# Cross-attention and expert layers on one core: attention inputs prepared a slot ahead, K and Q stacks by 6 writes and 4 reads, the gate with tokens as weights

## Chip, cores and metric

One core of one Trainium2 chip. The metric is device time in microseconds; the time of a version is the median of its runs.

## What is computed

```python
# x, ctx: (8, 256, 512) f32
h = layernorm(x, axis=-1)
q, k, v = Wq @ h + bq, Wk @ ctx + bk, Wv @ ctx + bv      # 256 channels = 16 heads of 16, 512 columns
p = softmax(scale * q^T k) per head                      # 512 x 512
x = x + tanh(g_xattn) * (Wo @ (p v) + bo)
# then, per token (a row of 512), 12 experts of width 320, the best 2 of each token:
t = layernorm(x);  logits = t @ gate_w.T;  cw = softmax weights of the top 2, renormalised
x = x + tanh(g_ffn) * sum_e cw[e] * (silu(t @ w1[e].T) * (t @ w3[e].T)) @ w2[e].T
```

## The kernel before

One program on one core. Its first part is attention, batch by batch, its second (routing, 43 tiles of 128 tokens by expert, an indirect scatter-add) works on all tokens.

**Slots.** Attention is a pipeline over 10 slots written out by `slots` (L343): in slot t (stage a) batch t is projected, (b_) batch t-1 has its scores, exponentials and products with V, (c) batch t-2 has its output projection, second normalisation and gate. Slots 2 to 7 are a loop of two. Slot 0 has only a, slot 1 a and b_, slot 8 b_ and c, slot 9 c. Each slot has 16 steps v (4 head groups by 4 blocks of 128 columns). In a step TensorE (`slot`, L1258) makes the two score groups of step v+1 (`scores`, two tiles S of 128x1024, each after the exponential that frees it), then the extra product that the table EXTRA (L322) puts there, then the products with V of step v (`values`, after the second exponential of step v). ScalarE makes two exponentials of 128x1024 in a step. The extra products are k0, k1, q0, q1 (a half of K or Q, 6 matmuls of 512 columns), v0, v1 (two blocks of V each), o0, o1 (output), t0, t1 (transposes of the normalised tokens), lg (gate logits as 12 x 256) and lt (their transposes through lgT).

**Products.** A projection uses weights and inputs split into a high and a low f16 part: three passes of two matmuls. VectorE makes the high part by a cast, GpSimd the low part by a subtraction (`lo_part`, L552, 2.1 us), and VectorE moves the results out of PSUM. All projections of a go through one PSUM tile MA, those of c through MC; each is used again only after VectorE has emptied it.

**K and Q.** Score matmuls contract over 49 rows: three blocks of 16 rows (K hi, hi, lo against Q hi, lo, hi) and a shift row. The stacks are built through DRAM: SP writes both parts of K (L469) and of Q (L471) with one DMA of 512 KB each, waits for both, and reads 12 blocks of 16 partitions x 8 KB in 1 KB runs (L480).

**Order on SP in a slot** (L425): load context and x of batch t; for c, row sums out of osum (L448), 4 of 8 moves of the sums of products, the inverse sums to DRAM (L453), the other 4, 8 broadcast reads of the inverse sums (L464); the writes and reads of K and Q; the stores of x and of the normalised tokens.

**Order on VectorE in a slot** (L812): bias into x (c); the quarter due at step 0; wait for the row sums, checks and reciprocal (L841, L843); cast of the context (L859), statistics of x (L861); then the steps: normalising x at step 2 (L886), the quotient at step 6 (L898), the evacuations, the token's second normalisation at step 11, osum after every fourth step (L965), and last the quarter due in this step.

**Quarters of expert weights.** Each of 12 experts has its weights split into f16 parts in four quarters (48 in all) beside attention: `split_quarter` (L791) on VectorE (L796, L798), and on ScalarE `store_quarter` (L665), which waits for the split, stores it and then issues the load of the quarter that uses the same buffer two quarters later (there are two buffers, c % 2). The store of a quarter split at step v stands behind the second exponential of step min(v + 2, 15):

```python
for v, e, c in splits:
    if u == 2 * min(v + 2, VS - 1) + 1:
        store_quarter(e, c)
```

A steady slot splits four, at steps 0, 5, 9 and 12; slot 0 four, slots 1 and 8 eight, slot 9 two, and the last two are split in the first expert tiles.

Of the kernel before, what the change touches and what calls it, by code (L numbers as in the profile page):

```python
# [14 lines left out]
P = 128  # L15
# [34 lines left out]
class Signals:  # L50


    def __init__(self, sem):
        self.xc = sem("xc")
# [38 lines left out]
def flamingo_kernel(nc, x, ctx_in, g_xattn, g_ffn, WqT, bq, WkT, bk, WvT, bv, WoT, bo, gateT, wall, out):  # L93
# [35 lines left out]
    q_dram = nc.dram_tensor("q_parts", [2, C, T], F16).ap()  # L129
    k_dram = nc.dram_tensor("k_parts", [2, C, T], F16).ap()  # L130
# [10 lines left out]
    with top:  # L141
# [13 lines left out]
        lgT = sb("lgT", [NE, C])  # L155
# [136 lines left out]
        s_rows = [sem(f"s_rows{i}") for i in range(2)]  # L292
        s_done = sem("s_done")

        def both_runs(eng, attention):
# [7 lines left out]
        NCONST2 = 3 + 3 + 1  # L303
# [14 lines left out]
        A_USES = {n: k for k, n in enumerate(("k0", "k1", "q0", "q1", "v0", "v1"))}  # L318
        C_USES = {n: k for k, n in enumerate(("o0", "o1", "t0", "t1", "lg", "lt"))}
# [6 lines left out]
        VS = GROUPS * TT  # L326

        def quarters(t):

            if t.i is None and t.add == 0:  # L330
                steps, experts = (4, 8, 11, 12), (0,)
            elif t.i is None and t.add == 1:
                steps, experts = (0, 2, 4, 6, 8, 10, 12, 14), (1, 2)
            elif t.i is None and t.add == B:
                steps, experts = (0, 2, 4, 6, 8, 10, 12, 13), (NE - 3, NE - 2)
            elif t.i is None and t.add == B + 1:
                steps, experts = (7, 7), (NE - 1,)
            else:
                steps, experts = (0, 5, 9, 12), (t.before(-1),)
            experts = [e if isinstance(e, At) else At(None, 0, e) for e in experts]  # L340
            return [(v, experts[n // 4], n % 4) for n, v in enumerate(steps)]

        def slots(eng, slot):  # L343

            slot(eng, At(None, 0, 0), 0, True, False, False)
            slot(eng, At(None, 0, 1), 1, True, True, False)
            with eng.Fori(0, (B - 2) // 2) as i:
                slot(eng, At(i, 2, 2), 0, True, True, True)
                slot(eng, At(i, 2, 3), 1, True, True, True)
            slot(eng, At(None, 0, B), 0, False, True, True)  # L350
            slot(eng, At(None, 0, B + 1), 1, False, False, True)
# [59 lines left out]
        def _(sp):  # L411
            sp.dma_start(w4[:, 0, :, :], WkT.rearrange("(k p) n -> p k n", p=P)).then_inc(s_const, 16)

            def attention(sp, g, guard):
# [4 lines left out]
                def load_batch(b, par):  # L419
                    sp.dma_start(ctx_sb[par][:, :, :],  # L420
                                 c_v[bass.ds(b.value(), 1)].rearrange("b p m t -> p (b m) t")).then_inc(g.xc, 16)
# [3 lines left out]
                def slot(sp, t, par, a, b_, c):  # L425
# [39 lines left out]
                    if a:  # L465

                        wait(sp, g.qk, t, 16 * 4 * PARTS, 0, s_bog)
                        wait(sp, g.kl, t, 1, 1)
                        sp.dma_start(k_dram.rearrange("h (m p) t -> p h m t", p=P), ks[:, :, :, :]).then_inc(g.qkst, 16)  # L469
                        wait(sp, g.ql, t, 1, 1)  # L470
# [34 lines left out]
            for n in range(2):  # L505
                sp.wait_ge(s_wst[n], 16 * 2 * (NE - 1))
            for e in range(EB // 2, NE):
# [7 lines left out]
                if e == NE - 1:  # L515
                    for n in range(2):
                        sp.wait_ge(s_wst[n], 16 * 2 * NE)
# [902 lines left out]
```

## Time and profile before

| | us |
|---|---|
| median of 3 runs | 808.91 (804.32 to 809.18) |
| the profiled execution | 802.83 |
| its span | 801.1 |

Times in rows are microseconds from the span's start, means of one instruction are ns. PE is TensorE's matmuls, PEld its weight loads, DVE VectorE, ACT ScalarE, POOL GpSimd, SP SyncE; a q behind the name (SPq, ACTq) is the engine's sequencer, which issues DMAs. "<-" behind a time in brackets names what ended the engine's idle time.

### The profile page before, as it was taken

The page shows a single profiled execution, that of the slowest core. Times are in us where ns is not written, and L with a number is a line of the kernel's source. Part 1 is how long each engine was busy: PE and PEld are TensorE (multiplying, and loading weights), DVE is VectorE, ACT ScalarE, POOL GpSimd, SP SyncE. Part 2 cuts the span into 40 slices and gives each one's busy share as a digit, 9 for nine tenths or more (in the row PEclk, how much of TensorE's full clock was granted, in tenths as well). Part 3 has the DMA queues.
Part 4 walks back from the last instruction along what each step waited for, and adds up shares of the span by engine and source line. Part 5 has one row for each costly group of instructions (what it writes and reads, how often), then busy time and mean ns, then how long its engine had stood idle before and what let it go on. Part 6 is the DMA issues. An engine that isn't in the chain of part 4 may idle for free.

```text
span 801.1 us, 14200 instructions
## 1 busy us (share of the span) xinstructions
PE 621.2 (78%) x4169; PEld 270.8 (34%) x4170; DVE 420.0 (52%) x769; ACT 332.0 (41%) x394; POOL 243.0 (30%) x186
## 2 busy tenths in 40 slices
PE   3418849889698897988976523179999999999993
PEld 1101202213122131322311101156666666666661
DVE  4787546667466574657646652944333333333330
ACT  5216637567565666665684200002222222222221
POOL 5203105133141332314202111324444333544322
PEclk9959969999999999999997755569999999999997
DMA  5686886967949688695894747527587776764533
GB/s 159 172 221 179 209 248 172 217 205 194 274 134 249 184 179 256 151 275 165 181 283 150 209 152 262 211 79 208 121 234 201 225 205 185 196 114 83 91 40 41
DMA packets 75374, 146.54 MB, mean 183 GB/s; under 512 B 10757, under 2 KB 36870, under 8 KB 73798
## 3 DMA queue, kind: packets, MB, share of 16 engines
q1 hardware_dynamic: 43664, 68.18, 31.4%
q10 hardware_dynamic: 22038, 55.35, 22.7%
q0 software_dynamic: 9632, 22.55, 14.9%
q8 instruction: 17, 0.28, 0.1%
q14 instruction: 23, 0.19, 0.1%
HBM read 87.85 MB, written 53.74 MB: 177 GB/s over the span
## 4 chain that ended last, share of the span: by engine, by line
PE 43%; DMA 19%; issue 16%; DVE 8%; POOL 5%; SPq 5%; ACT 1%; POOLq 0%; DVEq 0%; ACTq 0%
PE S L1334 15%; PE O L1355 9%; DMA K<-k_parts 8%; PE O L1198 5%; PE MA L1234 4%; DMA out<-yo,slot_out 4%; SPq L480 3%; PE S L1159 3%; DMA zl<-osum 2%; PE S L1321 2%; PE MC L1234 2%; DMA q_parts<-qs 2%; ACT prob L694 1%; PE S L1345 1%; POOL qs L552 1%
## 5 line engine op out<-in xcount | busy, mean ns | idle before, releaser
L694 ACT ACTIVATE prob<-S 128x1024 f32<-128x1024 f32 x256 | 245.8, 1024 | 179.8 <-PE S L1159 146.7
L1334 PE MATMUL S<-W,xT 128*128 x1032 | 149.4, 302 | 1.2 <-DVE xT L1107 1.2
L1198 PE MATMUL O<-prob,V 128*32 128x512 f32 x1024 | 148.1, 642 | 0.0
L1159 PE MATMUL S<-Q,K 49*128 49x512 f16 x512 | 91.4, 406 | 65.4 <-DMA K<-k_parts 42.2
L1334 PEld LDWEIGHTS S<-W,xT 128*128 128x128 f16 x1032 | 99.9, 99 | 38.7 <-issue 1.5
L620 POOL DMA_INDIRECT out<-yo,slot_out x43 | 68.5, 1593 | 116.9 <-DMA out<-yo,slot_out 60.0
L1355 PE MATMUL O<-W,hT 128*128 (+1 forms) x344 | 90.3, 381 | 0.9 <-DVE hT L1127 0.9
L1159 PEld LDWEIGHTS S<-Q,K 49*128 49x128 f16 x512 | 20.2, 94 | 193.6 <-ACT prob L694 135.4
L1115 DVE SCALAR_TENSOR_TENSOR hh<-S,act 128x320 f32<-128x320 f32 x43 | 21.1, 492 | 122.6 <-PE S L1334 122.6
L798 DVE SCALAR_TENSOR_TENSOR wp<-wf,wp 128x1024 f16<-128x1024 f32 x48 | 69.6, 1451 | 1.7
L552 POOL TENSOR_TENSOR cs<-ctx,cs 128x1024 f16<-128x1024 f32 x8 | 17.0, 2125 | 150.1 <-DVE cs L859 150.1
L596 POOL DMA_INDIRECT xg<-tokens_normed,slot_tok x43 | 42.6, 991 | 47.7 <-PE S L1321 35.3
L739 ACT ACTIVATE yo<-O,slot_w 128x512 f32<-128x512 f32 x43 | 29.6, 688 | 60.6 <-PE O L1355 60.6
L733 ACT ACTIVATE hs<-hh 128x320 f16<-128x320 f32 x43 | 20.2, 470 | 77.6 <-DVE hh L1115 77.6
L726 ACT ACTIVATE act<-S 128x320 f32<-128x320 f32 x43 | 18.8, 438 | 79.5 <-PE S L1334 79.5
L796 DVE TENSOR_SCALAR wp<-wf 128x1024 f16<-128x1024 f32 x48 | 41.2, 859 | 15.2 <-DMA wf<-wall 15.2
L1355 PEld LDWEIGHTS O<-W,hT 128*128 128x128 f16 (+1 forms) x344 | 31.6, 97 | 49.3 <-issue 29.0
L1234 PE MATMUL MA<-cs,w4s 128*128 128x512 f16 x96 | 28.3, 427 | 18.6 <-DVE kf L911 9.1
L1127 DVE COPY hT<-S 128x640 f16<-128x640 f16 x43 | 21.2, 492 | 41.0 <-PE S L1345 41.0
L552 POOL TENSOR_TENSOR os<-kf,os 128x1024 f16<-128x1024 f32 x8 | 17.8, 2229 | 77.1 <-DVE os L900 77.1
L1234 PE MATMUL MC<-os,w4s 128*128 128x512 f16 x96 | 27.6, 426 | 17.5 <-DVE os L900 13.7
L965 DVE COPY osum<-O 128x512 f32<-128x512 f32 x32 | 21.9, 685 | 30.0 <-PE O L1198 30.0
(153 smaller groups left out, 650.4 us busy)
## 6 DMA issues: line engine op xcount, KB each, us to landing
wf<-wall ACTq DMA_DIRECT2D x48, 512.0 KB, 7.1
weight_parts<-wp ACTq DMA_DIRECT2D x48, 512.0 KB, 4.7
W<-weight_parts SPq DMA_DIRECT2D x10, 2048.0 KB, 9.2
Q<-q_parts SPq DMA_DIRECT2D x48, 128.0 KB, 7.8
K<-k_parts SPq DMA_DIRECT2D x48, 128.0 KB, 8.2
ctx<-ctx_in SPq DMA_DIRECT2D x8, 512.0 KB, 12.5
residual<-x SPq DMA_DIRECT2D x8, 512.0 KB, 13.9
k_parts<-ks SPq DMA_DIRECT2D x8, 512.0 KB, 2.8
```

What stands on the lines that cost most here:

```text
L552: pool.tensor_tensor(parts[:, 1], f[:, :, :], parts[:, 0], ALU.subtract).then_inc(lo, 1)
L596: pool.indirect_dma_start(out=xg[j % TR][:, :], out_offset=None, in_=xn_dram[:, :], in_offset=bass.IndirectOffsetOnAxis(ap=slot_tok[:, j:j ...
L620: pool.indirect_dma_start(out=out[:, :], out_offset=bass.IndirectOffsetOnAxis(ap=slot_out[:, j:j + 1], axis=0), in_=yo[j % TR][:, :], in_o ...
L694: act.activation(prob[:, u % RING, :], S[u % 2][:, :], ACT.Exp, scale=SCALE).then_inc(g.exp, 1)
L739: act.activation(yo[n % TR][:, :], y_ps[:, :], ACT.Copy, scale=slot_w[:, bass.ds(j.value(), 1)])\
L796: dve.tensor_scalar(wp[c % 2][:, 0], wf[c % 2][:, :], WS, None, ALU.mult).then_inc(s_whi, 1)
L798: dve.scalar_tensor_tensor(out=wp[c % 2][:, 1], in0=wf[c % 2][:, :], scalar=WS, in1=wp[c % 2][:, 0], op0=ALU.mult, op1=ALU.subtract).then_ ...
L1159: last = pe.matmul(S[u % 2][:, s * T:(s + 1) * T], K[par][r0:r0 + PARTS * DK + 1, 2 * g4 + n, st * P:(st + 1) * P], Q[par][r0:r0 + PARTS * ...
L1198: last = pe.matmul(O[g4 % 2][2 * DK * j:2 * DK * (j + 1), :], V[par][:, st, GH * g4 + j, :], prob[:, u % RING, (j % 2) * T:(j % 2 + 1) * T ...
L1234: last = pe.matmul(bank[:, :], w4s[:, wp_, w, k, m * P:(m + 1) * P], src[:, xp, k, :], start=(n == 0 and k == 0), stop=(n == len(PASSES) - ...
L1334: last = pe.matmul(ps, xT[par][:, xp * TT + k, :], W[:, bass.ds(off + (w * WCOL + (2 * k + n) * F), F)], start=(k == 0 and (xp, w) == (0, 0)),
L1355: last = pe.matmul(y_ps[:, :], hT[par][0:rows_, block, :], W[0:rows_, bass.ds(off + (w * WCOL + W2 + k * T), T)], start=(n == 0), stop=(n ...
```

## The change

It does six things.

1. The pipeline gets a fourth stage p: in slot t the context and x of batch t+1 are loaded, x is normalised (statistics at step 6, values at step 8) and the context is cast (step 11). The loads have a semaphore each. Batch 0 is prepared before slot 0. The order on SP in a slot is now: loads of batch t+1, sums, K and Q, stores.
2. K, Q, V products move to steps 0 to 6 and 10, V in four pieces; the quotient goes to step 5, the second output product is cut in two halves (steps 8 and 9), the second normalisation goes to step 10. The extra product stands between the two score groups of a step. VectorE waits for the row sums at step 1 and takes the reciprocal before the range checks.
3. K and Q: 6 writes of 256 KB (one for each row block, each as soon as its part is there) and 4 reads of 48 partitions in 2 KB runs. The order of the heads changes with it (`head`), and Wo is loaded in 8 blocks. The shift row is used only in the second, guarded version of attention, so its 8 fills go from the main path.
4. The gate: tokens are the stationary operand, 8 products of 12 columns that give the logits directly; lt and lgT go.
5. Quarters: none in slots 0 and 9 and in the tiles, four in slot 1 (steps 4, 7, 11, 13), six in a steady slot (2, 4, 7, 11, 12, 13), eight in slot 8 as before.
6. At the start: context first, then Wk, then x; Wq and its biases ahead of Wv and Wo; the splits of Wk and Wq before slot 0; GpSimd's constants after the first low parts.

```diff
-        EXTRA = {3: "k0", 4: "k1", 5: "q0", 7: "q1", 8: "o0", 9: "v0", 10: "o1", 11: "v1", 12: "t0", 13: "t1",
-                 14: "lg", 15: "lt"}
-        ON_AT, XN2_AT, SPLIT_AT = 6, 11, 6
+        EXTRA = {0: "k0", 1: "k1", 2: "q0", 3: "q1", 4: "v0", 5: "v1", 6: "v2", 7: "o0", 8: "o1a", 9: "o1b",
+                 10: "v3", 12: "t0", 13: "t1", 14: "lg"}
+        ON_AT, LN_AT, XN_AT, XN2_AT, CS_AT, SPLIT_AT = 5, 6, 8, 10, 11, 3
...
         def quarters(t):
...
-                steps, experts = (0, 5, 9, 12), (t.before(-1),)
+                steps = (2, 4, 7, 11, 12, 13)
...
# SP, slot
-                    if a:
-
-                        wait(sp, g.xc, t, 32, 0, s_bog)
-                        wait(sp, g.a_free, t, NA, -NA)
-                        load_batch(t, par)
+                    if p:
+
+                        nxt = t.before(-1)
+                        wait(sp, g.cc, nxt, 16, 0, s_bog)
+                        wait(sp, g.xc, nxt, 16, 0, s_bog)
+                        wait(sp, g.cl, nxt, 1, -1)
+                        load_ctx(nxt, 1 - par)
+                        load_x(nxt)
...
+                        for stack, parts, dram, hi, lo, order in ((K, ks, k_dram, g.kh, g.kl, (0, 0, 1)),
+                                                                  (Q, qs, q_dram, g.qh, g.ql, (0, 1, 0))):
+                            wait(sp, hi, t, 1, 1)
+                            for r in sorted(range(PARTS), key=lambda r: order[r]):
+                                if order[r] == 1:
+                                    wait(sp, lo, t, 1, 1)
+                                sp.dma_start(dram[:, r], parts[:, order[r]].rearrange("p m t -> p (m t)"))\
+                                    .then_inc(g.qkst, 16)
...
+                        for stack, dram in ((K, k_dram), (Q, q_dram)):
+                            for s in range(2):
+                                sp.dma_start(stack[par][64 * s:64 * s + PARTS * DK, :, :]
+                                             .rearrange("p (g m) t -> p g (m t)", m=CT),
+                                             dram.rearrange("(g s) r c n -> s (r c) g n", s=2)[s]).then_inc(g.qk, 16)
...
# TensorE, slot
                     for v in range(VS):
                         if b_ and v + 1 < VS:
-                            scores(bb, 1 - par, v + 1)
-                        what = EXTRA.get(v)
+                            scores(bb, 1 - par, v + 1, (0,))
+                        what = EXTRA.get(v, "")
                         if a and what in A_USES:
                             project(t, par, what)
-                        if c and what in C_USES:
+                        if c and what[0:2] in C_USES:
                             output(bc, what)
+                        if b_ and v + 1 < VS:
+                            scores(bb, 1 - par, v + 1, (1,))
```

The DRAM tensors of K and Q parts are now `[8, 3, 16, 1024]` (heads in pairs of halves, row block, row, both halves of the columns' channels), so that `dram[:, r]` is 8 runs of 16 x 1024 values.

## Rows read from the trace of the kernel before

**Rows 1.** The page, part 4: shares of the chain that ended last, by engine.

```profile
PE 43%; DMA 19%; issue 16%; DVE 8%; POOL 5%; SPq 5%; ACT 1%; POOLq 0%; DVEq 0%; ACTq 0%
```

**Rows 2.** Busy time by stage: slots 0, 1, 4, 8, slot 0's end.

```profile
core 0: us, PE busy (x) PEld busy (x) DVE busy (x) ACT busy (x) POOL busy (x), PEclk, DMA share, GB/s
0.00:55.20 55.20, 16.68 (x52) 6.72 (x53) 36.29 (x43) 15.94 (x6) 15.24 (x24) 0.85 0.71 195
55.20:110.80 55.60, 37.72 (x232) 9.41 (x232) 32.21 (x38) 30.38 (x32) 10.18 (x6) 0.84 0.75 196
206.60:255.30 48.70, 40.19 (x270) 11.79 (x266) 30.67 (x50) 30.82 (x32) 14.61 (x10) 1.00 0.78 202
401.40:449.80 48.40, 36.51 (x220) 8.39 (x218) 29.68 (x39) 30.43 (x32) 6.88 (x4) 0.86 0.72 219
42.00:55.20 13.20, 0.00 (x0) 0.00 (x0) 10.63 (x5) 0.00 (x0) 0.00 (x0) 0.50 1.07 294
```

**Rows 3.** Timeline of slot 0: start, us, instruction, idle before it.

```profile
19.49 2.72 PE L1234 MATMUL MA<-xs,w4s 128*128 128x512 f16 x6 [0.89 <-issue]
...
20.75 3.02 DVE L798 SCALAR_TENSOR_TENSOR wp<-wf,wp 128x1024 f16<-128x1024 f32 x1
...
31.51 0.36 SPq L471 DMA_DIRECT2D q_parts<-qs  x1
...
34.29 0.33 SPq L480 DMA_DIRECT2D Q<-q_parts  x1
...
55.23 1.03 PE L1159 MATMUL S<-Q,K 49*128 49x512 f16 x4 [20.38 <-DMA K<-k_parts]
```

**Rows 4.** Timeline of a steady slot (slot 5), the same columns.

```profile
255.84 3.77 ACT L694 ACTIVATE prob<-S 128x1024 f32<-128x1024 f32 x4 [2.63 <-PE S L1159]
...
258.37 1.93 PE L1198 MATMUL O<-prob,V 128*32 128x512 f32 x8
...
265.35 2.13 POOL L552 TENSOR_TENSOR cs<-ctx,cs 128x1024 f16<-128x1024 f32 x1 [17.53 <-DVE cs L859]
...
268.76 3.59 SPq L464 DMA_DIRECT2D ocz<-inverse_sums  x8
...
273.33 0.61 PE L1159 MATMUL S<-Q,K 49*128 49x512 f16 x4
...
273.87 1.47 PE L1234 MATMUL MA<-xs,w4s 128*128 128x512 f16 x6
...
275.27 1.06 PE L1198 MATMUL O<-prob,V 128*32 128x512 f32 x8
...
276.78 1.94 ACT L694 ACTIVATE prob<-S 128x1024 f32<-128x1024 f32 x2 [0.99 <-PE S L1159]
...
279.64 1.94 ACT L694 ACTIVATE prob<-S 128x1024 f32<-128x1024 f32 x2 [0.92 <-PE S L1159]
...
304.34 0.73 PE L1159 MATMUL S<-Q,K 49*128 49x512 f16 x4 [1.92 <-DMA K<-k_parts]
```

**Rows 5.** DMA queues, 276:279 (first) and 255.3:304.2: packets, MB, share.

```profile
q1 hardware_dynamic: 528, 0.52, 49.3%
...
q10 hardware_dynamic: 1659, 4.18, 28.5%
```

**Rows 6.** Groups of the same slot, then the tile wf over the span.

```profile
L798 DVE SCALAR_TENSOR_TENSOR wp<-wf,wp 128x1024 f16<-128x1024 f32 x4 | 4.9, 1226 | 0.1
L796 DVE TENSOR_SCALAR wp<-wf 128x1024 f16<-128x1024 f32 x4 | 3.7, 932 | 0.0
...
DMA to landing us min/median/max: 4.1/7.1/13.8
```

**Rows 7.** Timeline of slot 9, then its chain in order of time.

```profile
470.78 1.03 PE L1234 MATMUL MC<-os,w4s 128*128 128x512 f16 x2 [0.63 <-POOL os L552]
...
473.58 0.74 DVE L935 SCALAR_TENSOR_TENSOR residual<-MC,cols,residual 128x512 f32<-128x512 f32 x1
...
484.41 8.10 DMA tokens_normed<-xs
```

More of the change, by code:

```diff
@@ L334, in quarters @@
             elif t.i is None and t.add == B:
-                steps, experts = (0, 2, 4, 6, 8, 10, 12, 13), (NE - 3, NE - 2)
-            elif t.i is None and t.add == B + 1:
-                steps, experts = (7, 7), (NE - 1,)
-            else:
-                steps, experts = (0, 5, 9, 12), (t.before(-1),)
-            experts = [e if isinstance(e, At) else At(None, 0, e) for e in experts]
-            return [(v, experts[n // 4], n % 4) for n, v in enumerate(steps)]
-        def slots(eng, slot):
[L345 to L351, printed above, removed]
+                steps = (0, 2, 4, 6, 8, 10, 12, 13)
@@ new lines, in quarters @@
+            return [(v, e, c) for v, (e, c) in zip(steps, parts)]
+        def slots(eng, slot):
+            slot(eng, At(None, 0, 0), 0, True, False, False, True)
+            slot(eng, At(None, 0, 1), 1, True, True, False, True)
+            with eng.Fori(0, (B - 4) // 2) as i:
+                slot(eng, At(i, 2, 2), 0, True, True, True, True)
+                slot(eng, At(i, 2, 3), 1, True, True, True, True)
+            slot(eng, At(None, 0, B - 2), 0, True, True, True, True)
+            slot(eng, At(None, 0, B - 1), 1, True, True, True, False)
+            slot(eng, At(None, 0, B), 0, False, True, True, False)
+            slot(eng, At(None, 0, B + 1), 1, False, False, True, False)
@@ L1147, in attention, with scores @@
             def attention(pe, g, guard):
-                def scores(b, par, v):
+                def scores(b, par, v, halves=(0, 1)):
                     g4, st = divmod(v, TT)
-                    if v == 0:
-                        wait(pe, g.qk, b, 16 * 4 * PARTS, 16 * 4 * PARTS)
-                    for n in range(2):
+                    if v == 0 and 0 in halves:
+                        wait(pe, g.qk, b, KQ_READS, KQ_READS)
+                    rows_ = PARTS * DK + (1 if guard else 0)
+                    for n in halves:
                         u = 2 * v + n
@@ L1230, in three @@
                             wait(pe, hi, b, 1, 1)
-                        if first and xp == 1:
+                        if first and xp == 1 and k == 0:
                             wait(pe, lo, b, 1, c)
-                        for k in range(CT):
-                            last = pe.matmul(bank[:, :], w4s[:, wp_, w, k, m * P:(m + 1) * P], src[:, xp, k, :],
-                                             start=(n == 0 and k == 0), stop=(n == len(PASSES) - 1 and k == CT - 1))
+                        last = pe.matmul(bank[:, :], w4s[:, wp_, w, k, m * P:(m + 1) * P], src[:, xp, k, :],
+                                         start=(n == 0), stop=(n == 3 * CT - 1))
                     return last
                 def output(b, what):
-                    wait(pe, g.c_free, b, NCU, C_USES[what] + 1, s_bias if what == "lt" else None)
-                    if what[0] == "o":
-                        m = int(what[1])
-                        last = three(MC, 3, m, os_, b, g.oh, g.ol, m == 0, 2)
-                    elif what[0] == "t":
-                        m = int(what[1])
+                    name, part = what[0:2], what[2:]
+                    n0, n1 = {"": (0, 3 * CT), "a": (0, 3), "b": (3, 3 * CT)}[part]
+                    if n0 == 0:
+                        wait(pe, g.c_free, b, NCU, C_USES[name] + 1)
+                    if name[0] == "o":
+                        m = int(name[1])
+                        last = three(MC, 3, m, os_, b, g.oh, g.ol, m == 0, 2, n0, n1)
+                    elif name[0] == "t":
+                        m = int(name[1])
                         wait(pe, g.xn2, b, CT, m + 1)
```

392 lines of the change are left out of this document (204 added, 188 removed).

## Prediction, made before the changed kernel was run

> **What bounds the kernel now.** I read the stages by windows first, then the chain, then a steady slot's timeline. The page's chain [rows 1] says that TensorE is on the path for 43% of the span and DMA for 19%. The windows [rows 2] give the stages: slot 0 takes 55.2 us with 16.68 us of TensorE work, slot 1 55.6 us, a steady slot 48.7 us (the one shown had the full clock and 40.19 us of TensorE work, 30.82 of exponentials, 30.67 of VectorE), slot 8 48.4 us. From 110.8 to 401.4 us six steady slots take 290.6 us, 48.4 us each. Routing, the expert tiles and the tail (from 491.5 us on) are not touched but for one expert's last two quarters.
>
> So no engine fills a steady slot. The timeline of one [rows 4] shows what does. VectorE waits for the row sums, casts the context only behind them, and GpSimd's low part of the context begins at 265.35 us, ten into the slot, after 17.53 us idle. K and Q are projected after that, written, read back, and the next slot's first scores at 304.34 us wait 1.92 us for K. A chain as long as the slot, not an engine, sets the period. In slots 0 and 1 the same chain is bare: the first scores come at 55.23 us after 20.38 us of waiting for K [rows 3].
>
> **Slot 0, -13 us.** The products for Q ended at 22.2 us (19.49 + 2.72), but VectorE was then in a 3.02 us split [rows 3]: no quarter is split in slot 0 now, which gives back 1.5 us; the context cast and the K weights no longer wait for x, about 1 us more. The last write of Q moves from 31.51 to some 29 us. The writes become six of 256 KB. A write of 512 KB in 1 KB packets took 49.3% of a 3 us stretch on 16 engines [rows 5], 1.5 us; K and Q together are 1.5 times as many bytes, but the last write is only half of the old one: 3 us to landing, as from 31.51 to 34.29 before, so the reads start at 32.3 us. Before, from the first read to the first scores it took 20.9 us (34.29 to 55.23) [rows 3], with a quarter's traffic and the next batch's loads beside it. Now these loads are done earlier, the packets are 2 KB and the DMAs four. Bounds: 20.9 us if none of that helps and, from below, 6 us, since 1.6 MB at the 294 GB/s of 42.0 to 55.2 us [rows 2] is 5.4 us. I take 9.7 us, nearer to the lower end because the loads beside it, 1 MB, and a quarter's 1 MB are more than the reads themselves: slot 0 ends at 42 us.
>
> The Trainium skill ("SBUF — State Buffer", the DMA port swizzle) says that the ports reached depend on the partitions of a transfer, eight partitions a port at 27.2 GB/s: 16 partitions reach 4 ports, 48 reach 8. By that the old reads need 14.5 us and the new ones 7.2, and slot 0 would end at 40 us. Against the change speaks "DMA: Bandwidth & Descriptors" (how many engines): the count divides the slowest dimension of both sides, which for the new writes is 8 on the DRAM side, so they would run on 8 engines, and the last write would take 0.7 us longer. No row here shows either.
>
> **Slot 1, -12.6 us.** Its K and Q products start at step 0 instead of step 3, since their inputs are ready; nothing waits for row sums. With q1 at step 3 the round trip fits in the remaining steps, so the wait for K at the end goes. What is late next is the pace. A step without a product is two exponentials (four in 3.77 us, so 1.88); one with a K, Q or output product is 0.54 + 1.40 + 1.00 = 2.94 us [rows 4]. Slot 1 has 4 of these (11.8), four V quarters at about 2.24 (9.0), eight bare steps (15.0): 35.8 us. A store and load issued on ScalarE stretches a bare step to 2.86 us (276.78 to 279.64) [rows 4]: 3.3 us for three bare steps and one with V. The clock is at its lower level after the idle stretch; a step there costs 1.03 (scores at 55.23) + 2.72 + 1.9 = 5.6 us [rows 3, 4] instead of 2.94, and part of the next: 3.9. Sum 43.0 against 55.6.
>
> **Slots 2 to 7, +1.6 us each.** TensorE's work is 40.2 us [rows 2]; the gate with tokens as weights replaces 4 products of 256 columns and two transposes by 8 products of 12 columns. Bounds 1 us either way; I take -0.7 (the turn through the narrow tile goes): 39.5. Extra products between the two score groups let ScalarE have its next input 1.4 us sooner, which keeps TensorE busy but doesn't shorten its work. Splits go from 4 to 6 quarters in a slot: each is 0.93 + 1.23 us on VectorE [rows 6] and one store and load on ScalarE. Their stores fall in steps 4, 6, 9, 13, 14, 15, none of which has a 1.40 us product: 3 x 0.6 (V and half-output steps) + 0.7 + 0.1 + 1.0 = 3.6 us. VectorE then has 34.5 us of work and holds up two things: V's third quarter behind the product of sums (1 us) and the second transpose behind two splits in steps 11 and 12 (1.7 us). Subtotal 45.8, rounded to 45.9.
>
> Then the term that speaks against the change. The sixth split is at step 13, and its buffer is the one of step 11: its load is issued by ScalarE only with the store of step 13. It lands 7.1 us later in the median, 4.1 to 13.8 [rows 6]; I take 6.5, since the reads are over. The split ends at 6.5 + 1.9 = 8.4 us after the issue. ScalarE's store of step 15 waits for it and stands in front of the next slot's exponentials. ScalarE gets there after four exponentials (4.1), another issue (1.0) and some 0.6 us of waiting: 5.7. So it stalls 2.7 us per slot, TensorE behind it idles, and its clock may drop for the next 6 us as at 258.37 us, where values took 1.93 instead of 1.06 us [rows 4]: 2.7 us if it does, 0 if it doesn't (it didn't in the slot at 206.6, whose clock was 1.00 [rows 2]); I take half. 45.9 + 2.7 + 1.4 = 50.0 us, against 48.4: +9.6 us for six. The row sums' wait hides inside this stall. DMA: the ACT queue's four quarters took 28.5% of a 48.9 us slot [rows 5], so six take 20.9 us of 50, seven more on a slot that had a DMA share of 0.78 [rows 2]: 0.9, close to full.
>
> **Slot 8, -2 us:** the same eight splits; the sums' round trip (output products had to wait for it) now runs without the tail of the reads; bounds -5 to +2 (the output product is a step earlier, so it can wait longer). **Slot 9, -4 us:** no split stands before the residual (it began at 473.58, its product was done at 471.81) and the two weight loads no longer start beside the last token store, which took 8.10 us [rows 7]; bounds -6 to -1. **Tiles:** the two quarters that go were hidden by TensorE's tiles: 0.
>
> **Sum.** 801.1 - 13.2 - 12.6 + 9.6 - 2 - 4 = 778.9 us of span; the profiled execution was 802.83 us, 1.7 above its span, so 780.6; the median of the runs is 808.91, 1.0076 times it: **787 us**.
>
> **Rivals.** (A) The forecast, 787; with the clock and load terms at their ends (48 to 53 us a slot) 774 to 805. (B) The late load costs nothing, because ScalarE and VectorE are themselves late when it lands: 45.9 us a slot, 3 x 6 = 15 less instead of 9.6 more: 762. For it: a load at the fast end, 4.1 us, would end the wait 2.4 us earlier, nearly all of the stall, and then no clock is lost. Against: the median is 7.1 us. (C) Slower: the queues are over-full at the slot's end. Context, x, the token store and a quarter's store are all in flight at step 13, and the load lands as the slow ones, 11.2 to 13.8 us [rows 6], 4.7 to 7.3 later than I took; at 55.5 us a slot the six cost 42.6 and all the gains (31.8) are eaten: 820. It decides from 53.7 us a slot, a landing of 10.2 us. For it: 0.9 of DMA share. Against: the reads of K and Q are over by step 12, so fewer transfers are beside this load than beside those issued late in a slot before. (D) The early preparation doesn't take the round trip off the slot's end, because the writes of K stand in SP's queue behind 17 transfers of sums (the last at 268.76 + 3.6, 15 us into the slot [rows 4]): slots as before, 48.4, and only the ends gain: 777. Against: 30 us remain for a round trip of 20.
>
> **How the numbers follow.** Chances: A 0.50, B 0.25, C 0.12, D 0.06, something else 0.07. Range for 8 in 10: from 757, a little below B, to 812, between A's end and C. A measurement tells about 1% from no change, so faster means under 800.8: nine tenths of A, all of B and D: 0.77. Within 1%: 0.13. Slower: C less its lower part: 0.10.
>
> **What would show it.** First exponential at about 42 us and the second batch's at 85; no wait for K at slot ends; a wait of scores' exponentials on a store issue at each slot's end, 2 to 3 us, with VectorE idle for the load before the last split; six slots of about 50 us. Wrong would be: reads of K and Q over 14 us, slots of 46 us or less (B), or loads landing over 10 us at step 13 (C).

## The result, and the profile after

The changed kernel took 819.4 us in the median of 4 runs (814.3 to 822.0); the kernel before, beside it on the same chip, 809.0. The ratio is 1.014, 95% interval 1.008 to 1.020: slower, where 787 us and faster were forecast. The profiled execution has a span of 812.5 us, 11.4 more than before; it was the fastest of the four runs. In a_spread three of the four runs and in x_dmaspr four of the eight, each time with the profiled one among them, took over 1.5% longer than the kernel's fastest run, so the slot figures of these two are the least sure.

I cut both spans at VectorE's last copy of row sums in each slot (osum), the same mark for all kernels below. "Rest" is slot 9, the routing, the tiles and the tail; slot 0 goes to the first exponential, slot 1 from there to its last copy.

| kernel | slot 0 | slot 1 | slots 2 to 7 | slot 8 | rest | span |
|---|---|---|---|---|---|---|
| before | 55.9 | 58.6 | 289.1 | 48.3 | 349.2 | 801.1 |
| after | 46.6 | 45.6 | 324.2 | 57.2 | 338.9 | 812.5 |

The ends gave what was hoped for, 9.3 + 13.0 + 10.3 us; the six steady slots took back 35.1 and slot 8 took 8.9. The six of both kernels, by windows (columns: engine busy time and instructions, granted TensorE clock, DMA share, GB/s). Before:

```profile
114.50:403.60 289.10, 249.81 (x1620) 72.14 (x1618) 184.22 (x302) 184.89 (x193) 87.71 (x60) 0.97 0.78 203
```

After:

```profile
92.20:416.40 324.20, 273.28 (x1656) 88.07 (x1654) 215.37 (x312) 188.67 (x191) 86.65 (x56) 0.89 0.79 227
```

Read TensorE first. Its work at full clock is the same: 249.81 x 0.97 = 242 and 273.28 x 0.89 = 243. Its idle time grew by 11.6 us (39.3 to 50.9); the other 23.5 of the 35.1 us are the same products at a lower granted clock, between the levels of 1.2 and 2.4 GHz. This is a division of time, not a price of the clock. The same stretch of two kernels below, a_oldq (the quarters of before) and x_both (hardly any split work and traffic), has slow products too, at 0.94 and 0.91, and these filled time in which TensorE had stood idle before:

```profile
110.10:400.00 289.90, 261.95 (x1657) 83.61 (x1656) 192.00 (x288) 190.94 (x194) 95.08 (x56) 0.94 0.76 214
90.50:374.40 283.90, 267.73 (x1656) 87.19 (x1656) 162.44 (x312) 189.62 (x193) 84.42 (x56) 0.91 0.58 137
```

With 12 and 18 us more of busy time than the kernel before, their six slots took 0.8 us more and 5.2 us less than its 289.1.

Where the stalls are, in the slot that answers to [rows 4] (255.3 to 310.4; the timeline of VectorE, GpSimd and ScalarE, start and duration first, in brackets the idle time before):

```profile
289.63 0.69 DVE L956 CAST xs<-xn 128x1024 f16<-128x1024 f32 x1
290.25 0.69 DVE L832 CAST cs<-ctx 128x1024 f16<-128x1024 f32 x1
290.85 0.68 DVE L964 COPY osum<-O 128x512 f32<-128x512 f32 x1
291.45 2.03 DVE L812 TENSOR_SCALAR wp<-wf 128x1024 f16<-128x1024 f32 x1
293.51 3.02 DVE L814 SCALAR_TENSOR_TENSOR wp<-wf,wp 128x1024 f16<-128x1024 f32 x1
...
306.82 0.69 DVE L812 TENSOR_SCALAR wp<-wf 128x1024 f16<-128x1024 f32 x1 [7.23 <-DMA wf<-wall]
...
290.41 2.52 POOL L596 TENSOR_TENSOR xs<-xn,xs 128x1024 f16<-128x1024 f32 x1 [1.85 <-DVE xs L956]
292.89 2.57 POOL L575 TENSOR_TENSOR cs<-ctx,cs 128x1024 f16<-128x1024 f32 x1
...
296.75 0.56 ACTq L697 DMA_DIRECT2D weight_parts<-wp  x1
297.47 0.53 ACTq L691 DMA_DIRECT2D wf<-wall  x1
298.18 1.94 ACT L716 ACTIVATE prob<-S 128x1024 f32<-128x1024 f32 x2 [5.12 <-issue]
...
309.00 0.56 ACTq L697 DMA_DIRECT2D weight_parts<-wp  x1
310.45 1.94 ACT L716 ACTIVATE prob<-S 128x1024 f32<-128x1024 f32 x2 [4.00 <-PE O L1229]
```

Two stalls stand there. **At step 11** VectorE casts two tiles, GpSimd subtracts twice behind the casts (290.41 to 295.46), and VectorE's split of a quarter lies across both: its two instructions take 2.03 and 3.02 us instead of 0.69 and 1.23. ScalarE's store (296.75) waits for that split in front of the exponentials: 5.12 us. **At step 13** the load issued at 297.47 lands some 9 us later, VectorE stands idle for 7.23 us, the split ends at 308.8, the store goes out at 309.00 and only then the next slot's exponentials run. The second is the late load of the forecast, with a slower landing; of the first the forecast had only 1.7 us for the transposes. Both splits are slow because of GpSimd: free ones take 0.69 and 1.23 us, and these two ended 0.55 and 1.07 us behind GpSimd's instructions, so they did most of their work only when those were over. Over the page (busy, mean ns, idle before; the last row the median landing):

```profile
L812 DVE TENSOR_SCALAR wp<-wf 128x1024 f16<-128x1024 f32 x48 | 48.6, 1012 | 48.9 <-DMA wf<-wall 48.9
L814 DVE SCALAR_TENSOR_TENSOR wp<-wf,wp 128x1024 f16<-128x1024 f32 x48 | 71.4, 1488 | 1.7
...
wf<-wall ACTq DMA_DIRECT2D x48, 512.0 KB, 7.1
```

VectorE's waits for loads rose from 15.2 us to 48.9. TensorE's and ScalarE's side of the same, the waits of slots 2 to 7 (total, times, longest), TensorE's for the transposes' copy before and after, ScalarE's after:

```profile
PE MC L1254 <- DVE xT L938: 7.0, 6, 1.2
...
PE MC L1280 <- DVE xT L933: 22.5, 6, 4.4
...
ACT prob L716 <- issue: 42.4, 12, 5.3
```

At the start, against [rows 3]: the last write of Q goes out at about 28.7, the reads at 33.25 and 34.12, and the first scores run at 45.92.

```profile
33.25 0.83 SPq L498 DMA_DIRECT2D K<-k_parts  x2
34.12 0.93 SPq L498 DMA_DIRECT2D Q<-q_parts  x2
...
35.17 0.40 SPq L432 DMA_DIRECT2D ctx<-ctx_in  x1
35.61 0.47 SPq L436 DMA_DIRECT2D residual<-x  x1
...
45.92 1.03 PE L1190 MATMUL S<-Q,K 48*128 48x512 f16 x4 [8.96 <-DMA Q<-q_parts]
```

### The profile page after: what moved, and what is told of

It is laid out like the page before. It is cut to its first block, busy times and chain, and to the rows that moved or that the text cites. A ratio compares the mean times of both kernels' runs of the same rounds, so it can differ in the third digit from the quotient of the medians.

```text
span 812.5 us, 13989 instructions
## 1 busy us (share of the span) xinstructions
PE 652.7 (80%) x4217; PEld 292.9 (36%) x4218; DVE 418.1 (51%) x757; ACT 324.0 (40%) x391; POOL 244.2 (30%) x186
## 3 DMA queue, kind: packets, MB, share of 16 engines
q10 hardware_dynamic: 22150, 55.35, 20.2%
## 4 chain that ended last, share of the span: by engine, by line
PE 48%; DMA 15%; DVE 15%; issue 11%; POOL 4%; SPq 3%; ACTq 1%; ACT 1%; DVEq 0%; POOLq 0%
PE S L1367 15%; PE O L1388 9%; PE O L1229 7%; DMA wf<-wall 5%; PE MA L1264 5%; PE S L1190 4%; DMA out<-yo,slot_out 3%; DVE wp L812 3%; DMA zl<-osum 2%; DVE wp L814 2%; PE S L1354 2%; PE MC L1284 2%; DMA ocz<-inverse_sums 1%; DMA Q<-q_parts 1%; PE MA L1246 1%
## 5 line engine op out<-in xcount | busy, mean ns | idle before, releaser
L716 ACT ACTIVATE prob<-S 128x1024 f32<-128x1024 f32 x256 | 252.1, 1025 | 207.9 <-PE S L1190 129.7
L1229 PE MATMUL O<-prob,V 128*32 128x512 f32 x1024 | 155.0, 682 | 0.0
L1190 PE MATMUL S<-Q,K 48*128 48x512 f16 x512 | 107.3, 425 | 43.7 <-ACT prob L716 33.0
L1190 PEld LDWEIGHTS S<-Q,K 48*128 48x128 f16 x512 | 24.3, 94 | 205.4 <-ACT prob L716 133.2
L812 DVE TENSOR_SCALAR wp<-wf 128x1024 f16<-128x1024 f32 x48 | 48.6, 1012 | 48.9 <-DMA wf<-wall 48.9
L814 DVE SCALAR_TENSOR_TENSOR wp<-wf,wp 128x1024 f16<-128x1024 f32 x48 | 71.4, 1488 | 1.7
L575 POOL TENSOR_TENSOR ks<-kf,ks 128x1024 f16<-128x1024 f32 x8 | 17.1, 2131 | 143.6 <-DVE ks L908 143.6
L761 ACT ACTIVATE yo<-O,slot_w 128x512 f32<-128x512 f32 x43 | 29.6, 688 | 60.6 <-PE O L1388 57.9
L1246 PE MATMUL MA<-w4s,cs 128*128 128x256 f16 x192 | 29.0, 291 | 16.1 <-DVE V L913 11.7
L1264 PE MATMUL MC<-os,w4s 128*128 128x512 f16 x96 | 28.9, 428 | 12.7 <-DVE os L890 11.0
L1280 PE MATMUL MC<-ident,xn 128*128 128x128 f32 x64 | 14.1, 360 | 27.3 <-DVE xT L933 23.3
```

The source lines that it names most:

```text
L575: pool.tensor_tensor(parts[:, 1], f[:, :, :], parts[:, 0], ALU.subtract).then_inc(lo, 1)
L716: act.activation(prob[:, u % RING, :], S[u % 2][:, :], ACT.Exp, scale=SCALE).then_inc(g.exp, 1)
L812: dve.tensor_scalar(wp[c % 2][:, 0], wf[c % 2][:, :], WS, None, ALU.mult).then_inc(s_whi, 1)
L814: dve.scalar_tensor_tensor(out=wp[c % 2][:, 1], in0=wf[c % 2][:, :], scalar=WS, in1=wp[c % 2][:, 0], op0=ALU.mult, op1=ALU.subtract).then_ ...
L1190: last = pe.matmul(S[u % 2][:, s * T:(s + 1) * T], K[par][r0:r0 + rows_, 2 * g4 + n, st * P:(st + 1) * P], Q[par][r0:r0 + rows_, 2 * g4 + ...
L1229: last = pe.matmul(O[g4 % 2][2 * DK * j:2 * DK * (j + 1), :], V[par][:, st, head(g4, j), :], prob[:, u % RING, (j % 2) * T:(j % 2 + 1) * T ...
```

## The experiments

The question was why a steady slot takes 54.0 us (324.2 / 6) where 48.2 were needed before. The slot figures below are all of this kind, from each kernel's one profile; the medians are of all its runs. Runs of one kernel differ by some 8 us, so a difference of 1 us in a slot (6 us over six) tells nothing.

**a_spread, a_noint, a_oldq, b_late: the place, the order or the number of the quarters.** The edits:

```
a_spread:  -steps = (2, 4, 7, 11, 12, 13)   +steps = (0, 3, 5, 8, 10, 13)
a_noint:   -scores(bb, 1 - par, v + 1, (0,)) ... scores(bb, 1 - par, v + 1, (1,))
           +scores(bb, 1 - par, v + 1)      (the product behind both groups)
a_oldq:    the quarters of before: slot 0 (4, 8, 11, 12), slot 1 eight, slots 2 to 7 (0, 5, 9, 12),
           slot 8 eight, slot 9 (5, 6, 7, 8)
b_late:    kernel before:  -steps = (0, 5, 9, 12)   +steps = (0, 11, 12, 13)
```

> The changed kernel with the same six quarters in a steady slot, split at steps 0, 3, 5, 8, 10, 13 instead of 2, 4, 7, 11, 12, 13, so that each load has two steps or more between its issue and its split. Theory T (the place of the quarters: the load for the split at step 13 is issued at step 13, and a second pile-up on VectorE at step 11): a slot goes from 54.4 to 49 to 51 us, the whole from 819 to 788 to 798, and ScalarE no longer waits for the store at a slot's end. Rival N (six quarters are too many for the engines and the DMA, wherever they stand): a slot stays at 53.5 us or more and the whole at 814 or more. Rival G (products between the score groups, the gate's new form, or the new writes and reads of K and Q are what lengthens the slot): as rival N, within 3 us of 819.

> The changed kernel with the extra product of a step again behind both score groups of the next step, nothing else. Theory T: the slot's length is set by the waits at steps 11 and 13, so the order of products inside a step does little: 816 to 822. Rival G in the form that the products between the groups cost (exponentials now come singly): a slot loses 1.5 us or more of its 54.4, the whole is under 811. If the order gains what its place suggests (ScalarE has its next input 1.4 us sooner), taking it away costs 3 to 10 us: 822 to 829.

> The changed kernel with the quarters laid out as before the change: 4 in slot 0 (steps 4, 8, 11, 12), 8 in slot 1, 4 in each of slots 2 to 7 at steps 0, 5, 9, 12, 8 in slot 8 and 4 in slot 9 (steps 5 to 8). Everything else of the change stays. Theory T and rival N both: a steady slot falls from 54.4 to 47 us or less, the six by 44 us or more, slots 0, 1 and 9 give back some 15: 785 to 795. Rival G: a slot stays at 51 us or more and, with slots 0, 1 and 9 longer, the whole is 812 or more.

> The kernel before with its four quarters of a steady slot split at steps 0, 11, 12, 13 instead of 0, 5, 9, 12, nothing else: the same number of quarters, but the load for the last one is issued at step 13, as in the changed kernel. Theory T: a slot gets 3 to 6 us longer than its 48.35, the whole goes from 809 to 827 to 845, with the wait for a store at the slot's end. Rival N: the number is the same, so the time is: within 4 us of 809.

a_spread: 819.7 us (806.7 to 822.7), 55.6 us a slot. Even its fastest run lies above the 798 that theory T allowed: T as I had put it fell. a_noint: 822.5 us, ratio 1.023 (1.016 to 1.031), 55.9 a slot: the products between the score groups cost nothing; if anything they gain some 3 us, which the intervals do not separate. a_oldq: 805.1 us, ratio 1.000 (0.997 to 1.004), 48.3 a slot, with slot 0 at 55.7 and slot 1 at 54.4. Everything else of the change (early preparation, writes and reads, gate) is in it, so rival G fell for the steady slots: the 5.7 us came with the two extra quarters and their new steps. But those parts gained nothing there either, 289.9 us for the six against 289.1, and the whole lies between what T and N said (785 to 795) and what G said (812). Of a_oldq's 12 quarters in slots 0 and 1, eight more than in the changed kernel, the cost is (55.7 + 54.4) - (46.6 + 45.6) = 17.9 us, 2.2 each. b_late: 844.0 us, ratio 1.046 (1.039 to 1.054), 55.4 a slot with only four quarters. So three late steps are worth 7.2 us a slot, where I expected 3 to 6. They hold two things, a late load and three splits in a row; TensorE's waits in the six slots (112.8 to 444.9) have both, 34.9 us for the copy behind the split that waits for its load and 20.2 us for the transposes' copy (7.0 before):

```profile
PE MC L1250 <- DVE lgT L940: 34.9, 6, 6.7
PE MC L1247 <- DVE xT L938: 20.2, 6, 3.4
```

Its VectorE rows, with split times as before the change and a wait for the load:

```profile
319.39 1.23 DVE L798 SCALAR_TENSOR_TENSOR wp<-wf,wp 128x1024 f16<-128x1024 f32 x1
329.38 0.69 DVE L796 TENSOR_SCALAR wp<-wf 128x1024 f16<-128x1024 f32 x1 [8.17 <-DMA wf<-wall]
```

So by these profiles six quarters at well-spaced steps cost as much as six at bad ones, and four at bad steps as much as both. What they share had to be found.

**x_dve, x_dma, x_store, x_pool: one resource taken away at a time.**

```
x_dve:    both instructions of a split on [0:64] of 1024 columns
x_dma:    loads wf[:, 0:64] (not the first two), stores of 64 columns (not expert 0's); experts read expert 0's parts
x_store:  only the stores cut, as in x_dma
x_pool:   GpSimd's subtractions on [..., 0:32] of 512 columns
(x_dve and x_pool fill the rest of the parts with zeros once at the start)
```

> The changed kernel with the two VectorE instructions of a split cut from 1024 to 64 columns (the experts' weights are then mostly not split; all loads, stores, their order and their waits stay). Two theories of why a steady slot takes 54 us with six quarters and 48 with four. Theory V (VectorE is late: splits of 1.9 us, stretched to 3.7 where GpSimd subtracts beside them, stand in front of what the products and ScalarE's stores wait for): the slots fall to 45 to 48 us, 36 us or more for the six. Theory D (DMA: the traffic of 1 MB a quarter and the landing of the loads): the slots stay above 52 us.

> The changed kernel with the loads and stores of quarters cut to 64 of 1024 columns, except the first two loads and the stores of expert 0 (the experts then all read the first one's parts; the same issues on ScalarE, the same work on VectorE). Theory D: the slots fall to 46 to 48 us. Theory V: the loads are never late any more, which takes off the 2 to 3 us of the wait for the last load, but VectorE's stretched splits stay: 50 to 52 us a slot.

> The changed kernel with only the stores of quarters cut to 64 columns (except those of expert 0; all experts read its parts). Half of the added traffic goes. Theory D in the form of bandwidth: a slot falls by 3 us or more, the median landing of the loads from 7.1 to under 5.5 us. Theory V: under 2 us a slot.

> The changed kernel with GpSimd's subtractions of the low parts cut from 512 to 32 columns each (the low parts are then mostly zero; six memsets of GpSimd are added at the start). Theory V with the lock between GpSimd and VectorE as its main part: no split instruction takes over 1.3 us, VectorE's busy time falls by 9 us or more a slot and a slot to 49 to 51 us. If the lock is a side matter: a slot stays above 52.5 us. Theory D: above 53.

x_dve: 813.7 us, ratio 1.007 (1.003 to 1.012), 55.6 a slot: against theory V as far as it is the splits' own work, for the hold-up by GpSimd stays (below). x_dma: 784.7 us, ratio 0.972 (0.966 to 0.979), 50.9 a slot: against D, inside what V said. x_store: 797.0 us, 52.9 a slot, median landing 6.5, so not D in the form of bandwidth (3 us or more and under 5.5). x_pool: 810.3 us, ratio 1.005 (1.001 to 1.009), 55.1 a slot, above the 52.5 that I had set for "a side matter", though its split instructions are all free of GpSimd:

```profile
L818 DVE SCALAR_TENSOR_TENSOR wp<-wf,wp 128x1024 f16<-128x1024 f32 x48 | 58.8, 1225 | 1.7
L816 DVE TENSOR_SCALAR wp<-wf 128x1024 f16<-128x1024 f32 x48 | 32.9, 686 | 63.4 <-DMA wf<-wall 63.1
```

The waits in the last row tell where the gain went: the time won on VectorE was waited for the loads, 63.1 us in place of 48.9 (in x_dve 70.6). The loads also landed later, 8.2 us in the median and in x_dve 8.9, for 7.1; why was not tried. x_dve also shows that the stretch has nothing to do with the size of the split: at step 11 even 64 columns took 1.53 and 2.08 us, 1.35 and 1.85 more than free ones (0.18 and 0.23), where 1024 columns took 1.34 and 1.79 more. They end right behind GpSimd's instructions (295.57 + 2.52 = 298.09, 298.06 + 2.11 = 300.17).

```profile
296.61 1.53 DVE L814 TENSOR_SCALAR wp<-wf 128x64 f16<-128x64 f32 x1
298.18 2.08 DVE L816 SCALAR_TENSOR_TENSOR wp<-wf,wp 128x64 f16<-128x64 f32 x1
```

```profile
295.57 2.52 POOL L596 TENSOR_TENSOR xs<-xn,xs 128x1024 f16<-128x1024 f32 x1 [1.85 <-DVE xs L958]
298.06 2.11 POOL L575 TENSOR_TENSOR cs<-ctx,cs 128x1024 f16<-128x1024 f32 x1
```

The Trainium skill states this in "SBUF — State Buffer" (SBUF: two separate sides): VectorE, in an instruction of a two-port mode or with two inputs from SBUF, and GpSimd share a pair of ports by an exclusive lock, and whichever starts second is blocked until the first is through. The trace agrees: a 0.18 us instruction took 1.53.

**a_lfirst, a_lfspr, c_mix, b_lfirst: the load ahead of its store.** ScalarE issued a quarter's store and then the next load into the same queue.

```
a_lfirst, b_lfirst:   -act.dma_start(w_dram[...], wp[...])   load_quarter(e, c + 2)
                      +load_quarter(e, c + 2)   act.dma_start(w_dram[...], wp[...])
a_lfspr:              the same, steps (0, 3, 5, 8, 10, 13)
c_mix:                the same; slot 0 none, slot 1 eight, slots 2 to 5 (0, 5, 9, 12), slots 6 and 7 (0, 2, 5, 7, 9, 12),
                      slot 8 eight, one quarter in slot 9 at step 7, three behind the first three tiles
```

> The changed kernel with the two DMAs that ScalarE issues for a quarter in the other order: the next load first, the store behind it (both in one queue, 512 KB each). Theory D in the form of landing (a load lands late because it stands behind its own store in the queue): the median landing falls from 7.1 to 5.5 us or less, the stalls of the step-13 load shrink by 1.5 us or more a slot, and the whole goes from 819 to 810 or less. Theory D in the form of bandwidth (16 DMA engines share out what is in flight): the landing stays within 0.7 us and the time within 4 us of 819.

> The changed kernel with both: loads issued before stores, and the six splits at steps 0, 3, 5, 8, 10, 13. With loads of 5.5 us or less each one is there when its split's turn comes (two or three steps of 3 us), so the landing form of theory D says 50 us or less a slot and 795 or less in all. The bandwidth form: as a_spread, 815 to 822.

> A version made to beat both: the changed kernel, loads before stores, four quarters at steps 0, 5, 9, 12 in slots 2 to 5, six in slots 6 and 7 (0, 2, 5, 7, 9, 12), eight in slots 1 and 8, none in slot 0, and of the last expert one quarter in slot 9 and three behind the first three tiles, where VectorE, ScalarE and the DMAs have room. By the stages measured so far: slot 0 47, slot 1 54, slots 2 to 5 48 each, 6 and 7 53 each, slot 8 54, the rest 341 to 344: 794 to 798 of span, 798 as the median; if the order of load and store also tells, 790.

> The kernel before with only the order of load and store turned round. Four quarters in a slot at steps 0, 5, 9, 12 leave their loads at least 7 us, so both forms of theory D say little: landing form 802 to 807 against 809, bandwidth form the same as before within 3 us.

a_lfirst: 814.1 us, ratio 1.009 (1.005 to 1.013), median landing 5.7 for 7.1: the loads did stand behind their stores, but little over half of the expected 9 us came, and in its profile the steady slots took 54.0 us as before. VectorE's waits before a split were now for an earlier store to leave its buffer, 45.5 us where it had waited 48.9 for loads. b_lfirst: 802.6 us, ratio 0.995 (0.992 to 0.999), landing 5.5: a swap of two lines that makes the kernel before a little faster. a_lfspr: 812.1 us, 54.5 a slot: with loads in time, the spread layout was still no good. c_mix: 809.4 us, far above the 798 expected: slots 6 and 7 took 54.9 each, and slot 9 with the routing was 75.5 us long with its one quarter, against 70.2 in c_t4 below without it, while three quarters behind the tiles cost 1.5 us (261.9 to 260.4).

**x_both, x_dmaspr, c_t4, c_t11: both at once, and the tiles.**

```
x_both:    x_dve and x_dma together
x_dmaspr:  x_dma with steps (0, 3, 5, 8, 10, 13)
c_t4:      as c_mix, nothing in slot 9, the last expert's four quarters behind tiles 0 to 3
c_t11:     the last eleven quarters behind tiles 0 to 10; slot 1 (2, 5, 8, 11, 14), slots 2 to 7 (0, 5, 9, 12), slot 8 eight
```

> The changed kernel with both cuts together: the two split instructions on 64 of 1024 columns, and loads and stores of quarters of 64 columns (except the first two loads and the stores of expert 0). With VectorE's part alone cut a steady slot stayed at 55.6 us, with the DMAs' part alone at 50.9. Theory S (a slot's end is late by the later of two things, VectorE behind its splits and the loads' landing, so only both cuts together free it): 45 to 47 us a slot, 276 or less for the six. Theory D (only the DMAs count): 50 to 51 us, as with the DMAs' cut alone.

> The changed kernel with small loads and stores as before and the six splits at steps 0, 3, 5, 8, 10, 13; VectorE's work is whole. Theory S: without traffic the place of the splits counts, since nothing is then late but VectorE at steps 11 to 13: 47 to 49 us a slot against 50.9 with the change's steps, and with full traffic (54.5 to 55.6 in this place) the rest is the DMAs' share: 6 us a slot for six quarters, 1 us each. If VectorE's total work (six splits of 2.5 us) is what binds: 50.5 or more.

> Loads before stores, four quarters in slots 2 to 5, six in 6 and 7, eight in 1 and 8, none in 0 and 9, and the last expert's four quarters behind the first four tiles. The earlier version with one quarter in slot 9 and three in the tiles took 809.4 us; its slot 9 and routing were 9.5 us longer than with no quarter there, its tiles 1 us. Both theories: that goes, 798 to 802. If a quarter costs its 3 us in the tiles too: 807 or more.

> The same with the last eleven quarters behind the first eleven tiles, so that five are in slot 1, four in each of slots 2 to 7 and eight in slot 8. By stages: slot 0 46, slot 1 46, the six 290, slot 8 52, slot 9 and routing 66, tiles and tail 275: 775 us of span, 777 as the median, if a quarter is free in the tiles (six steps of 1 us each there). If it costs 3 us there: 800. For this routing the experts come late enough; a routing that needs the last two experts in the first tiles would have to wait for them, so this run shows what the place is worth.

x_both: 762.0 us, 47.3 a slot. Alone the cuts moved a slot by +1.6 and -3.1 us, together by -6.7: theory S, one stall hides the other. What x_both takes away on VectorE is the splits' own work; in slots 2 to 7, 17 of its 72 split instructions still lose 22.5 us beside GpSimd's. x_dmaspr: 809.8 us (797.8 to 816.0), ratio 0.998 (0.994 to 1.003), 55.0 a slot, where S said 47 to 49. With hardly any traffic the spread layout was 4 us a slot worse than the change's own, and even its fastest run is 13 us above x_dma's 784.7, so its limit is not the traffic. Its timeline has what I take for the reason, four times in a slot; here step 10:

```profile
298.01 0.69 DVE L957 CAST xs<-xn 128x1024 f16<-128x1024 f32 x1
298.62 0.69 DVE L813 TENSOR_SCALAR wp<-wf 128x1024 f16<-128x1024 f32 x1
299.34 3.03 DVE L815 SCALAR_TENSOR_TENSOR wp<-wf,wp 128x1024 f16<-128x1024 f32 x1
```

```profile
298.78 2.51 POOL L596 TENSOR_TENSOR xs<-xn,xs 128x1024 f16<-128x1024 f32 x1 [1.85 <-DVE xs L957]
```

VectorE's cast releases GpSimd's subtraction, and a split in the same step stands right behind the cast: it is held up nearly every time. Between 85 and 480 us, 25 split instructions were stretched in a_spread, by 43.7 us in all; some 20 and 27 us in the changed kernel, some 10 and 11 before, none in x_pool. My spread steps 3, 5, 8 and 10 were the very steps with a cast. But a stretch costs only where something waits for it: in slots 2 to 7, a_oldq has 22.5 us of it and c_t11 22.6, as much as the changed kernel (23.7), and their slots took 48.3 and 47.7 us. In a_oldq TensorE waited only 3.9 us in all for the transposes' copy.

c_t4: 802.4 us, ratio 0.995 (0.991 to 0.999). c_t11: 785.6 us, ratio 0.976 (0.971 to 0.981): 47.7 a slot, and the tiles 270.8 us for 260.4, so eleven quarters cost 10.4 us there, 0.9 each, against 2 to 3 in the slots. This layout relies on a routing in which the last experts come late.

**a_clear and c_clear4: steps without a cast.**

```
a_clear:   a_lfirst with steps (0, 2, 4, 7, 9, 13)
c_clear4:  a_clear; slot 1 (4, 7, 10, 13), slot 8 (0, 4, 9, 13), the last expert's four quarters behind tiles 0 to 3
```

> The changed kernel with loads before stores and the six splits at steps 0, 2, 4, 7, 9, 13: at none of these does VectorE cast something in the same step (K at 1, Q at 3, the attention output at 5, x at 8, the second x at 10, the context at 11), so GpSimd's subtraction of 2.1 to 2.6 us is over before the split begins, and each load has two steps or more. Theory L (the splits stand right behind a cast, whose subtraction on GpSimd locks them out; late loads are the other half): no split instruction over 1.3 us for most, VectorE's busy time 6 us less a slot than in a_lfspr, and a slot falls from 54.5 to 48 to 50 us, the whole from 812 to 780 to 790. Theory S alone (VectorE's total or the traffic of six quarters binds, wherever they stand): 53 us or more a slot, 808 or more in all.

> The version before with slot 8 relieved: loads before stores, six splits in each of slots 2 to 7 at steps 0, 2, 4, 7, 9, 13, four in slot 1 (4, 7, 10, 13), four in slot 8 (0, 4, 9, 13), and the last expert's four quarters behind the first four tiles. Against 795.3 us: slot 8 gets 6 to 10 us shorter (four quarters less), slot 9 and the tiles 4 us longer together, as in c_t4 (3.7 and 0.8): 789 to 793. If VectorE's order and the loads are what counts, slots 2 to 7 stay at 51 to 52 us. If the gain of the version before was chance, they go back to 54 and the whole to 805.

a_clear: 795.3 us, ratio 0.989 (0.984 to 0.994), 51.6 a slot: the first layout of six quarters that beats the kernel before; against the changed kernel only the place of the splits and the order of two DMAs are new. It stopped 1.6 us a slot above what theory L said (48 to 50), and 795.3 is above its 780 to 790. Against a_lfspr, with the same order of DMAs, VectorE was busy for 29.6 us less in the six slots (230.8 to 201.2) and the slots were 17.5 us shorter. That it is the hold-up by GpSimd and not other work of VectorE at the same steps was not tried apart: no run took GpSimd's subtractions from the spread layout. The rows of its page and its waits in slots 2 to 7:

```profile
L814 DVE SCALAR_TENSOR_TENSOR wp<-wf,wp 128x1024 f16<-128x1024 f32 x48 | 62.4, 1300 | 1.7
L812 DVE TENSOR_SCALAR wp<-wf 128x1024 f16<-128x1024 f32 x48 | 42.5, 885 | 13.6 <-DMA weight_parts<-wp 13.2
```

```profile
ACT prob L716 <- issue: 9.1, 4, 4.0
```

ScalarE's waits in front of a store fell from 42.4 us to 9.1, and VectorE's before a split from 48.9 to 13.6, nearly all for a store to free its buffer. What is late next stands in TensorE's waits of the same stretch:

```profile
PE MA L1246 <- DVE V L913: 19.9, 6, 4.6
...
PE MA L1264 <- DVE kf L901: 8.2, 5, 4.1
```

The copies of V come late behind the split of step 4, which stands in front of them in VectorE's order, and those of K behind the wait for the row sums. c_clear4: 787.8 us, ratio 0.978 (0.972 to 0.984), 51.7 a slot, slot 8 40.6 us, slot 9 and routing 68.1. It holds for any routing: a token goes to two different experts, so at least half of all pairs, hence over four tiles, come before the last expert's. It and c_t11 are the best versions found, equal within the intervals.

## Why the prediction was wrong

**The direction came from the steady slots.** The sum said 45.9 + 2.7 + 1.4 = 50.0 us; 54.0 were measured, which over six slots is 24 of the 34 us that separate the forecast span (778.9) from the real one.

- *The stall by the late load, 2.7 us* (landing 6.5): the mechanism was right, the size was not. In the slot shown the load took 9.3 us, VectorE stood for 7.23, ScalarE for 4.00; over the six slots the load of step 13 took 6.8 to 11.6 us. b_late, with its three splits in a row, was 7.2 us a slot longer. Rival C named this at 0.12, with its point at 10.2 us of landing; one of the six loads reached that. That the time it gave, 820, came true is luck, because the next term failed too. Nor were the queues over-full: the DMA share of the six slots was 0.79, not 0.9.
- *VectorE's hold-ups, 1 + 1.7 us, and splits at 0.93 + 1.23 each*: this is the step that failed. The 0.93 of [rows 6] already mixed free instructions (0.69 us) with one that stood beside GpSimd's; the 1.23 was that of free ones. I carried both over to a layout that puts a split right behind the context cast moved to step 11. There the pair took 5.05 us, and TensorE waited 3.8 us a slot for the transposes' copy, ScalarE 5.12 us for the store, a wait that the sum put at nothing. No rival named it. How the missing 4.0 us divide between this term and the load's is open, because they hide each other: x_pool, with no split held up, got nothing back. That both together are the cause is what x_both (47.3) and, with whole work and traffic, a_clear (51.6) show.
- *The clock, 1.4 us*: the granted clock of the six went from 0.97 to 0.89, 23.5 us of slow products or 3.9 a slot. What of it lengthened the slots is not shown: x_both had 0.91 and slots of 47.3 us.
- *Rival B* (the load is hidden behind others' lateness, 762) was half right and in the wrong sense: the two do hide each other (x_dve, x_pool), but as two full stalls, not as none. That x_both took 762.0, B's own number, is luck: it also leaves out 53 us of VectorE's work in the six slots.

**Slot 0, -13 us**: -9.3. The writes landed at 33.2 instead of 32.3; the reads took 12.7 us (33.25 to 45.92), not 9.7. From 35 us on the DMAs were busy for over 0.9 of the time, and from 36 to 45 us they moved 135 to 182 GB/s, where my lower bound had 294. The Trainium skill's rule ("SBUF — State Buffer", the DMA port swizzle) gives an estimate of 7.2 us for the reads, further off than my 9.7; 1 MB of other loads was queued behind them. **Slot 1, -12.6**: right, -11.4 by first exponentials and -13.0 by the copies, although one of its loads took 12.4 us. **Slot 8, -2**: +8.9. Its eight splits were taken as unchanged, and they are the same in most runs here, whose slot 8 lies anywhere from 46.2 us (x_dve) to the 57.2 of this profile; a_noint has 50.8. So one profile says little about it, and what made the 8.9 us was not tried. c_clear4 took four quarters away and has 40.6. **Slot 9, -4**: right in sign; it and the routing gained 10.5, of which the last token store, without weight loads beside it, gave 2.9 (5.2 us for 8.1), as its term said; the rest was not followed. **Tiles, 0**: right, 261.0 against 260.4. **Rival D** is contradicted for the round trip (no wait for K or Q in slots 2 to 7 but one of 1.4 us), yet its number was nearest for the steady slots once the quarters were as before: a_oldq, 48.3.

## What to carry to other kernels

When an instruction is moved in one engine's order, look at what the instruction ahead of it releases on the engine that shares its port, and cost it by its blocked time, not by a mean over both kinds. When two stalls stand in one stage, taking one away can show nothing; cut both before calling either harmless. A slow instruction is a cost only if something waits for it. And a DMA issue that waits inside the stream of the engine that feeds the bottleneck is priced by its worst landing, with the load put ahead of the store in the queue.

## What the runs showed of the hardware

- A blocked VectorE instruction does most of its work when GpSimd's is over, so the loss hardly depends on its size: 64 columns took 1.53 and 2.08 us where free ones take 0.18 and 0.23, 1024 columns 2.03 and 3.02 where free ones take 0.69 and 1.23.
- A load issued behind a 512 KB store in its own queue landed 1.4 to 1.6 us later in the median than one issued ahead of it (7.1 to 5.7 and 7.1 to 5.5), and the store then took 7.6 us instead of 4.9 and 6.7 instead of 4.7: the load's gain was the store's loss, and a little more.
- A lower granted clock need not cost time where TensorE has idle time to fill: six slots with 262 us of TensorE work at a clock of 0.94 (a_oldq) took 289.9 us, six with 250 us at 0.97 (before) 289.1.
- A DMA issue on ScalarE, 0.5 us as a rule, took up to 2.2 us in the attention part of the changed kernel, in front of the exponentials.
